# S4 kernel and context projections moved into earlier stages, answers and two norms in one stage, key shifts one group ahead

## The chip, the cores and the metric

The kernel runs on one core of a Trainium2 chip, with its five engines: TensorE (PE), VectorE (DVE), ScalarE (ACT), GpSimd (POOL) and SyncE (SP, which issues most transfers). The metric is the time of one execution in microseconds, the median of several runs.

## The reference

Two decoder layers on 8 sequences of 256 tokens with 256 features; each of six parts is added to x and followed by a norm.

```python
x = _layernorm(x + _L0_attn_ref(x, ...))             # selective scan
x = _layernorm(x + _L0_xattn_ref(x, ctx_768, ...))
x = _layernorm(x + _L0_ffn_ref(x, gate_w, w1, w2))   # 16 experts, one per token, 160 places each
x = _layernorm(x + _L1_attn_ref(x, ...))             # starts with layer_norm(x, ln1_scale, ln1_bias)
x = _layernorm(x + _L1_xattn_ref(x, ctx_768, ...))   # top 32 of the context, then an S4 convolution
x = _layernorm(x + _L1_ffn_ref(x, ...))              # product keys, 4096 experts
# of the expert part:   ans = einsum('tec,ecd->td', combine_weights, expert_out)
# of the top-32 part:   K = x_vision @ Wk;  V = x_vision @ Wv   (they depend on the context alone)
#   s4d:                K = 2 * einsum('dn,dnl->dl', dC, powers).real   (depends on weights alone)
# of the product keys:  q = (q - mean) * rsqrt(var + eps) * gamma + beta;  sim = q . keys
```

## The kernel before, in words

The 2048 tokens are 16 tiles of 128 rows in a buffer X, with a transposed copy XT. The kernel is a row of stages. Each stage is one block, in which every engine has a program of its own, written out in order and tied to the others by semaphores; between blocks all engines meet at a barrier. There is no scheduler. The order of the code is the order of each engine's queue, SP's and POOL's too.

**Routing** (`moe_route`, from L1359): TensorE makes the gate's logits and counts tokens by expert (L1423, L1424), VectorE ranks them and then computes small factors of the S4 kernel (`factor_step`), POOL scatters the 16 tiles to `moe_dispatch` in DRAM (L1489), ScalarE makes phases of the S4 tables.

**Experts** (`moe_experts`, L1494): for each of 16 experts TensorE does a first layer (L1573), turns the next expert's tokens (L1546) and the previous answers back (L1556), and a second layer (L1586). ScalarE and VectorE evacuate; SP loads weights two experts ahead and stores answers. Beside them ScalarE (`scalar_step`) and POOL (`gpsimd_program`) make the S4 tables UU and VV.

**Combine** (`norm_only` with `beside=Combine`): TensorE makes the S4 kernel as 256 products of UU and VV (L1312), VectorE copies it to KA (L1328), SP moves KA to KB in 16 transfers (L1305), TensorE transforms it (L1322) and VectorE copies the filter to KF (L1334). POOL gathers the experts' answers by token (L1291). VectorE adds them to X (L1298), behind its copies, and norms X (L442 to L450, L408).

**Performer** (`stage_performer`): a norm of X to X1 with the transposed copy in XT, a block in which POOL fills parts of VA with ones (L1735), then the projections (`products`, L204), where TensorE fills eight banks in turn and VectorE evacuates them. Later the inputs of the top-k attention are loaded (`topk_inputs`): context, weights, masks.

**Top-k attention** (`topk_attention`): projections of 4 query, 4 key and 16 value jobs (L204, copied by L238 and L239), with a norm of X beside them on VectorE and POOL (L362); then a block of two mask operations (L1998), then the attention.

**Product keys**: `norm_gram` norms X and accumulates a Gram matrix on TensorE (L2417), six tiles behind the turning (LAG); POOL centres its input (L2396). `peer_sides` handles 16 heads in 4 groups of 4. For a group, TensorE spreads the Gram matrix (L2524), VectorE accumulates variances (L2616) and makes scales, POOL scales keys (L2674), TensorE folds keys and shift (L2532, L2539), ScalarE copies, TensorE turns (L2548), ScalarE copies to WP (L2596). The shift is split into three bfloat16 rows BR by six operations of POOL (L2681 to L2686). Then come 8 units of 2 tiles: products of XT and WP and one of BR (L2562, L2563), which VectorE scans for the largest 8 (L2641, L2645). Groups 0 and 1 are accumulated ahead of the loop, group g + 2 in the loop of group g.

## Time and profile before

| | us |
|---|---|
| median of 3 runs | 2572.31 |
| lowest, highest | 2571.13, 2576.33 |
| the profiled execution's own time | 2596.7 |
| its span | 2594.9 |
| PE, DVE busy in the span | 2206.9 (85%), 1668.3 (64%) |
| ACT, POOL busy | 920.4 (35%), 884.3 (34%) |

The mean granted clock of TensorE is 0.925 of full speed. Matmuls are pipelined, so a busy share of PE is not the share of its peak. The page's own chain of waits (its part 4) follows the end of the program back through the last stage only, and shows 0% of the span for each engine, so the stages have to be read one at a time.

### The profile page before, as it was taken

How to read it: one execution, taken by the hardware profiler on the slowest of the kernel's cores; microseconds unless marked ns; L12 is line 12 of the kernel's file. 1: busy time of each engine (PE TensorE's matmuls, PEld its weight loads, DVE VectorE, ACT ScalarE, POOL GpSimd, SP SyncE). 2: the span in 40 equal slices, each digit the busy share in tenths (PEclk: the TensorE clock that was granted, in tenths of full speed). 3: DMA queues.
4: the chain of work that ended last, by engine and by line, in shares of the span. 5: the costliest groups of instructions: out<-in, count | busy, mean ns of one | idle time of the engine just before them, and what ended most of it. 6: DMA issues, size and time to landing. Idle time of an engine off the chain costs nothing. (4 is left out here: it accounts for less than half of the span.)

```text
span 2594.9 us, 34470 instructions
## 1 busy us (share of the span) xinstructions
PE 2206.9 (85%) x12574; PEld 1516.8 (58%) x12574; DVE 1668.3 (64%) x4342; ACT 920.4 (35%) x1840; POOL 884.3 (34%) x529
## 2 busy tenths in 40 slices
PE   8788888998964993898996777869778989999997
PEld 3355555634644992465473444325655678888886
DVE  6799999415662125456045999360547788888886
ACT  2498898215845210135312443023110222122220
POOL 0298887004508953132102333340421111111110
PEclk9899999999987996899997888879898999999998
DMA  3121111000033662100100000020030000000000
GB/s 98 54 70 49 50 49 37 11 0 1 1 116 116 231 222 61 49 2 2 39 21 19 1 1 1 0 87 25 1 130 1 3 1 1 1 1 1 1 1 33
DMA packets 59003, 103.07 MB, mean 40 GB/s; under 512 B 8082, under 2 KB 39698, under 8 KB 57684
## 3 DMA queue, kind: packets, MB, share of 16 engines
q1 hardware_dynamic: 57300, 96.69, 11.1%
q0 software_dynamic: 1536, 4.20, 0.5%
q8 instruction: 100, 1.64, 0.3%
q14 instruction: 67, 0.55, 0.1%
HBM read 91.04 MB, written 9.57 MB: 39 GB/s over the span
## 5 line engine op out<-in xcount | busy, mean ns | idle before, releaser
L762 POOL TENSOR_TENSOR XT<-mamba_DU,scan_BS 128x1024 f32<-128x1024 f32 x128 | 299.2, 2360 | 148.3 <-DMA scan_BS<-mamba_rows 110.8
L891 DVE TENSOR_TENSOR_SCAN scan_H<-scan_AB,XT 128x512 f32<-128x512 f32 x256 | 296.3, 1209 | 8.1 <-POOL XT L762 4.9
L2784 PE MATMUL ex_HP<-XT,pe_DOWN 128*128 128x256 f32 x1024 | 249.3, 390 | 5.8 <-PEq L2513 5.0
L2815 PE MATMUL ex_OP<-pe_UP,ex_GH 128*128 128x256 f32 x1024 | 231.5, 380 | 0.0
L2784 PEld LDWEIGHTS ex_HP<-XT,pe_DOWN 128*128 128x128 f32 x1024 | 194.0, 194 | 31.4 <-issue 5.1
L821 ACT ACTIVATE scan_AB<-mamba_E,mamba_AA 128x510 f32<-128x510 f32 x256 | 198.7, 776 | 37.9 <-DVE scan_H L891 33.5
L776 PEld LDWEIGHTS scan_TP<-ident,scan_H 128*128 128x128 f32 x1024 | 120.1, 142 | 157.3 <-DVE scan_H L891 81.2
L2845 ACT ACTIVATE ex_GH<-ex_HP 128x512 f32<-128x512 f32 x128 | 76.5, 599 | 380.4 <-PE ex_HP L2784 345.7
L2815 PEld LDWEIGHTS ex_OP<-pe_UP,ex_GH 128*128 128x128 f32 x1024 | 194.0, 190 | 26.1
L785 PE MATMUL scan_YT<-mamba_BC,ident 128*128 128x512 f32 x384 | 198.4, 599 | 4.1 <-ACT scan_YS L837 2.3
L776 PE MATMUL scan_TP<-ident,scan_H 128*128 128x128 f32 x1024 | 147.6, 278 | 46.0 <-DVE scan_H L891 46.0
L2871 POOL TENSOR_TENSOR ex_AS<-ex_AS,pe_IV 128x512 f16<-128x512 f16 x32 | 52.9, 1684 | 363.0 <-DVE ex_AS L2919 363.0
L2896 DVE TENSOR_TENSOR ex_L<-ex_IOTA,ex_KEYS 128x4096 f16<-128x4096 f16 x64 | 151.8, 2372 | 2.2
L830 ACT ACTIVATE mamba_BC<-scan_TP,scan_CT 128x512 f32<-128x512 f32 x192 | 129.6, 675 | 3.9 <-PE scan_TP L776 3.9
L2970 DVE SCALAR_TENSOR_TENSOR ex_GH<-ex_GP,ex_GH 128x1024 f32<-128x1024 f32 x64 | 78.4, 1225 | 61.0 <-issue 32.4
L1630 DVE TENSOR_SCALAR experts_HT<-experts_HP 128x320 f32<-128x320 f32 x32 | 15.7, 492 | 132.2 <-PE experts_HP L1573 132.2
L2562 PE MATMUL sides_SP_<-sides_WP,XT 128*128 128x256 f32 x256 | 79.8, 439 | 19.7 <-POOL sides_BR L2686 19.7
L2050 PE MATMUL tk_TP<-tk_DG,tk_PP 128*128 128x128 f32 x256 | 55.2, 403 | 47.3 <-ACT tk_DG L2143 47.3
L2804 PEld LDWEIGHTS ex_GP<-ex_R,ex_L 128*128 128x128 f16 x2048 | 77.8, 117 | 15.6 <-DVE ex_L L2896 4.7
L2050 PEld LDWEIGHTS tk_TP<-tk_DG,tk_PP 128*128 128x128 f32 x256 | 52.0, 311 | 54.9 <-ACT tk_DG L2143 54.9
L2804 PE MATMUL ex_GP<-ex_R,ex_L 128*128 128x32 f16 x2048 | 77.6, 191 | 7.5 <-DVE ex_L L2896 3.9
L1586 PE MATMUL experts_YT<-experts_HT,moe_W 128*128 128x160 f32 x512 | 76.2, 309 | 8.0 <-ACT experts_HT L1602 7.4
(452 smaller groups left out, 4553.6 us busy)
## 6 DMA issues: line engine op xcount, KB each, us to landing
moe_W<-in_L_ffn_w SPq DMA_DIRECT2D x32, 1024.0 KB, 7.5
scan_BS<-mamba_rows SPq DMA_DIRECT2D x64, 256.0 KB, 3.1
pe_DOWN<-in_L_ffn_down SPq DMA_DIRECT2D x1, 4096.0 KB, 12.3
pe_UP<-in_L_ffn_up SPq DMA_DIRECT2D x1, 4096.0 KB, 21.7
moe_dispatch<-s4t_BOTH SPq DMA_DIRECT2D x1, 2560.0 KB, 8.7
experts_XE<-moe_dispatch SPq DMA_DIRECT2D x16, 160.0 KB, 2.4
moe_answers<-experts_YE SPq DMA_DIRECT2D x16, 160.0 KB, 3.5
XT<-in_xT SPq DMA_DIRECT2D x4, 512.0 KB, 5.8
```

What stands on the lines that cost most here:

```text
L762: pool.tensor_tensor(BU[:, r % 2, cs], tokens(DU, cs, r // DS), row, ALU.mult).then_inc(bu_ready, 1)
L776: ins = pe.transpose(TP[:, i % SLOTS, c * P:(c + 1) * P], H[:, r % 2, c, tb * P:(tb + 1) * P], ident[:, 0:P])
L785: pe.matmul(YT[:, tb, :], ident[:, 0:P], HT[:, n % 4, :], start=(s == 0), stop=(s == DS - 1)).then_inc(y_added, 1)
L821: act.activation(later(AB[:, n % 2, :]), later(tokens(E, c, g)), ACT.Exp, scale=AA[:, 2 * c, s:s + 1], bias=AA[:, 2 * c, s:s + 1]).then_in ...
L830: act.activation(HT[:, n % 4, :], TP[:, item(r, tb) % SLOTS, :], ACT.Copy, scale=CT[:, TB * g + tb, s:s + 1]).then_inc(act_read, 1)
L891: v.tensor_tensor_scan(H[:, r % 2, c], AB[:, n % 2, :], BU[:, r % 2, c], 0.0, ALU.mult, ALU.add).then_inc(h_ready, 1)
L2050: ins = pe.matmul(TP[:, n % 2, 0, k * P:(k + 1) * P], PP[:, n % 2, h, k * P:(k + 1) * P], DG[:, h, :], start=(h == 0), stop=(h == XH - 1))
L2562: pe.matmul(SP_[:, n % BANKS, a, :], XT[:, k, t * P:(t + 1) * P], WP[:, k, keys], start=(k == 0), stop=False)
L2784: ins = pe.matmul(HP[:, n % 2, a, :], DOWN[:, k, 2 * q + a, :], XT[:, k, b * BLK:(b + 1) * BLK], start=(k == 0), stop=(k == KD - 1))
L2804: ins = pe.matmul(GP[:, n % 2, t, :], L[:, n % 2, t // RUN, :, t % RUN], R[:, n % 2, t // RUN, :, t % RUN], start=True, stop=True)
L2815: ins = pe.matmul(OP[:, m % 2, 0:D], GH[:, b % 2, j, a * P:(a + 1) * P], UP[:, j, :], start=(j == 0), stop=(j == J2 - 1))
L2896: v.tensor_tensor(L[:, n % 2], numbers(P), along(0, P), ALU.is_equal).then_inc(left_ready, 1)
```

## The change

The keys and values of the context (`ContextProducts`) are made in the routing, into space of the S4 tables, stored in DRAM during the experts and loaded as inputs of the top-k attention. ScalarE's two power steps move from behind experts 0 and 1 to behind experts 2 and 3, and wait for these stores. The S4 kernel is made in two chunks beside experts 14 and 15, four tiles of TensorE's columns at a time, two channels a product, and stored in DRAM (`s4_kernel`) in 16 transfers; the space for it on PSUM comes from YT, which has one bank instead of two. The combine stage and the performer's first norm become one (`combine_norms`), in groups of 2, 4, 4, 4 and 2 tiles; X1 is normed straight from the sum, by a variance with both epsilons, and X itself is normed by ScalarE beside the projections (`LateNorm`). The filter's transform is four more jobs of those projections. The Gram products go three tiles behind. In `peer_sides` the accumulation goes one group ahead, and the split of the shift is two copies on ScalarE and two operations on VectorE.

```diff
+class ContextProducts:
...
+    def tensor(self, pe):
+        self.loads.wait(pe)
+        for n in range(self.count):
+            if n >= self.RING:
+                pe.wait_ge(self.read, n - self.RING + 1)
+            bank = self.ring[:, n % self.RING, :]
+            if n < self.keys:
+                for k in range(2):
+                    ins = pe.matmul(bank, self.WK[0:KC[k], k, :], self.CT[0:KC[k], k, n * G4:(n + 1) * G4], start=(k == 0), stop=(k == 1))
+            else:
+                for a in range(2):
+                    t = 2 * (n - self.keys) + a
+                    for k in range(2):
+                        ins = pe.matmul(bank[:, a * D:(a + 1) * D], self.CT[0:KC[k], k, t * P:(t + 1) * P], self.WV[0:KC[k], k, :],
+                                        start=(k == 0), stop=(k == 1))
+            ins.then_inc(self.ready, 1)
+    def vector(self, v, first, last):
+        for n in range(first, last):
+            v.wait_ge(self.ready, n + 1)
+            bank = self.ring[:, n % self.RING, :]
+            if n < self.keys:
+                v.tensor_copy(self.KT[:, n * G4:(n + 1) * G4], bank).then_inc(self.read, 1)
+            else:
+                t = 2 * (n - self.keys)
+                v.tensor_copy(self.V[:, t:t + 2, :], bank.rearrange("p (a d) -> p a d", a=2)).then_inc(self.read, 1)
...
     def scalar_step(self, act, n):
-        if n == 1:
+        if n == 3:
+            act.wait_ge(self.space_free, 32)
             self.powers(act, self.HIGH, self.AR, ACT.Exp, LO).then_inc(self.moduli_ready, 1)
-        elif n == 2:
+        elif n == 4:
...
                 tables.load(sp)
+                context.loads.issue(sp)
                 sp.wait_ge(zero_ready, 1)
...
                 ch.link(v.tensor_tensor(WT[:], SM[:], KEEP[:], ALU.mult))
+                v.wait_ge(zeroed, 16)
+                context.vector(v, 0, 1)
                 for n in range(3):
                     tables.factor_step(v, n)
+                    context.vector(v, 2 * n + 1, 2 * n + 3)
+                context.vector(v, 7, context.count)
...
+                    if e == 1:
+                        sp.dma_start(io["topk_keys"], context.KT).then_inc(tables.space_free, 16)
+                        sp.dma_start(io["topk_values"], context.V).then_inc(tables.space_free, 16)
...
+                for n in range(CHUNKS):
+                    if n == CHUNKS - 1:
+                        store(NE - 2)
+                    sp.wait_ge(kernel_copied, n + 1)
+                    for j in range(TILES):
+                        for a in range(PAIR):
+                            r, d = j * KN + a * HI, n * P + j * KN + a * KI
+                            sp.dma_start(kernel[:, :, d:d + KI].rearrange("l h d -> h l d"), KA[r:r + HI, n, a]).then_inc(kernel_stored, 16)
                 store(NE - 1)
...
+                def kernel_products(n):
+                    pe.wait_ge(tables.factors_ready, 1)
+                    if n:
+                        pe.wait_ge(kernel_copied, n)
+                    for i in range(KI):
+                        for j in range(TILES):
+                            d = slice(n * P + j * KN + i * PAIR, n * P + j * KN + (i + 1) * PAIR)
+                            ins = pe.matmul(KP[j * KN:(j + 1) * KN, i * PAIR * LO:(i + 1) * PAIR * LO], tables.UU[:, d, :].rearrange("p a h -> p (a h)"),
+                                            tables.VV[:, d, :].rearrange("p a l -> p (a l)"), start=True, stop=True)
...
                         turn_back(e - 1)
+                    if e >= FIRST_CHUNK:
+                        kernel_products(e - FIRST_CHUNK)
                     pe.wait_ge(relu_act, 2 * (e + 1))
                     pe.wait_ge(relu_dve, 2 * (e + 1))
-                    if e >= 2:
-                        pe.wait_ge(ys_copied, e - 1)
+                    if e:
+                        pe.wait_ge(ys_copied, e)
...
+                def kernel_out(n):
+                    v.wait_ge(kernel_ready, n + 1)
+                    v.tensor_scalar(KA[:, n].rearrange("p a l i -> p i a l"), KP[:].rearrange("p (i a l) -> p i a l", a=PAIR, l=LO), 2.0, None, ALU.mult).then_inc(kernel_copied, 1)
...
+class LateNorm:
...
+    def scalar(self, act):
+        for t in range(NT):
+            act.activation(self.X[:, t, :], self.X[:, t, :], ACT.Identity, scale=self.RS[:, 0, t:t + 1], bias=self.NB[:, t:t + 1])
...
+def combine_norms(nc, name, late, X1, XT, ident, GA, ones, rest, scale, bias, loads, ahead):
...
+    GROUPS = (slice(0, 2), slice(2, 6), slice(6, 10), slice(10, 14), slice(14, 16))
...
+            @block.gpsimd
+            def _(pool):
+                for g in range(NG):
+                    for t in tiles(g):
+                        pool.indirect_dma_start(out=GA[:, t, :], out_offset=None, in_=rest.answers,
+                                                in_offset=bass.IndirectOffsetOnAxis(ap=rest.FROM[:, t:t + 1], axis=0)).then_inc(gathered[g], 16)
+                pool.memset(ones, 1.0)
+            @block.sync
+            def _(sp):
+                loads.issue(sp)
+                landed(sp, 2)
+                for a in ahead:
+                    a.issue(sp)
+            @block.vector
+            def _(v):
+                ch = Chain(v, dve_chain)
+                for g in range(NG + 1):
+                    if g < NG:
+                        landed(v, g)
+                        for t in tiles(g):
+                            ins = v.scalar_tensor_tensor(X[:, t, :], GA[:, t, :], rest.WT[:, t:t + 1], X[:, t, :], ALU.mult, ALU.add)
+                        ch.link(ins)
+                        for t in tiles(g):
+                            ins = v.bn_stats(raw[:, t, :], X[:, t, :])
+                        ch.link(ins)
+                        for t in tiles(g):
+                            ins = v.bn_aggr(MV[:, t, :], raw[:, t, :])
+                        ch.link(ins)
+                        v.tensor_scalar(RS[:, 0, GROUPS[g]], MV[:, GROUPS[g], 1], 1.0, 1e-5, ALU.mult, ALU.add)
+                        v.tensor_scalar(RS[:, 1, GROUPS[g]], MV[:, GROUPS[g], 1], 1.0 + 1e-6, 1e-11, ALU.mult, ALU.add).then_inc(var_ready, 1)
+                    if g:
+                        of = GROUPS[g - 1]
+                        v.wait_ge(std_ready, g)
+                        v.reciprocal(RS[:, :, of], RS[:, :, of]).then_inc(scale_ready, 1)
+                        v.wait_ge(scale_ready, g)
+                        for t in tiles(g - 1):
+                            v.tensor_scalar(X1[:, t, :], X[:, t, :], MV[:, t, 0:1], RS[:, 1, t:t + 1], ALU.subtract, ALU.mult).then_inc(normed, 1)
+                        v.scalar_tensor_tensor(NB[:, of], MV[:, of, 0], -1.0, RS[:, 0, of], ALU.mult, ALU.mult)
...
+                     (MASK[:], io["causal"]), (KEPS[:], io["L1_attn_key_eps"]), (WK_[:], io["dft_kernel"])] +
+                     [(KB[l * HI:(l + 1) * HI], inputs.kernel[l::LB].rearrange("i h d -> h i d")) for l in range(LB)])
...
+            for q in range(NF):
+                jobs.append((KF[:, q, :], [(WK_[:, i, q, :], KB[:, i, :]) for i in range(LO // LB)], by_channel))
+            products(nc, "pfproj", jobs, loads, dve_only=True, ahead=[mlp_loads], beside=late, evictor_needs=[loads])
             performer_core(nc, ident, QT, KT, VA, MASK, X1)
...
-                jobs.append((KT[:, tok], [(WK[0:KC[k], k, :], CT[0:KC[k], k, tok]) for k in range(2)], copy_out))
-            for t in range(NT):
-                jobs.append((V[:, t, :], [(CT[0:KC[k], k, t * P:(t + 1) * P], WV[0:KC[k], k, :]) for k in range(2)], copy_out))
             products(nc, "tkproj", jobs, inputs.loads, ahead=[film_loads], beside=NormBeside(nc, s2, X, Z, ident))
...
-    LAG = 6
+    LAG = 3
...
-                for c in range(2 * CG):
+                for c in range(CG):
...
-                        if g + 2 < NGR and u < ACCUMULATE_TO:
-                            spread((g + 2) * CG + u)
+                        if g + 1 < NGR and u < ACCUMULATE_TO:
+                            spread((g + 1) * CG + u)
...
+                    act.activation(B0[0:3, :], BP[0:3, 0:CK], ACT.Copy)
+                    act.activation(BH[0:3, 0, :], BP[0:3, 0:CK], ACT.Copy).then_inc(bias_copied, 1)
                     act.wait_ge(folded, g + 1)
                     act.activation(WT_[:, g % 2], WTP[:], ACT.Copy).then_inc(folded_copied, 1)
+                    act.wait_ge(rest_ready, g + 1)
+                    act.activation(BH[0:3, 1, :], BX[0:3, :], ACT.Copy).then_inc(rest_copied, 1)
                     act.wait_ge(turned, g + 1)
...
+                def bias_rest(g):
+                    v.wait_ge(bias_copied, g + 1)
+                    v.scalar_tensor_tensor(BX[0:3, :], BH[0:3, 0, :], SPLIT[0:3, 0:1], B0[0:3, :], ALU.mult, ALU.add).then_inc(rest_ready, 1)
+                def split_bias(g):
+                    v.wait_ge(rest_copied, g + 1)
+                    v.scalar_tensor_tensor(BR[0:3, g * CK:(g + 1) * CK], BH[0:3, 1, :], SPLIT[0:3, 1:2], BX[0:3, :], ALU.mult, ALU.add).then_inc(bias_split, 1)
...
-                def split_bias(g):
-                    b, x, h = B0[0:3, g % 2, :], BX[0:3, :], BH[0:3, :]
-                    pool.wait_ge(bias_copied, g + 1)
-                    for n in range(2):
-                        ch.link(pool.tensor_copy(h, b if n == 0 else x))
-                        if n == 0:
-                            ch.link(pool.tensor_scalar(x, h, SPLIT[0:3, 0:1], None, ALU.mult))
-                            ch.link(pool.tensor_tensor(x, b, x, ALU.subtract))
-                    ch.link(pool.tensor_scalar(b, h, SPLIT[0:3, 1:2], None, ALU.mult))
-                    pool.tensor_tensor(BR[0:3, g * CK:(g + 1) * CK], x, b, ALU.subtract).then_inc(bias_split, 1)
-                    pool.wait_ge(bias_split, g + 1)
```

VectorE's program from the end of the experts on, before. KA is the S4 kernel's copy, s_GA the gathered answers, RS the reciprocal deviations.

```order
L1328 TENSOR_SCALAR combine_KA<-combine_KP 16x32x16 x8
L1298 SCALAR_TENSOR_TENSOR X<-s_GA,moe_WT,X 128x256 x4
L442 BN_STATS moenorm_raw<-X 128x6 x4
L445 BN_AGGR moenorm_MV<-moenorm_raw 128x2 x4
L1298 SCALAR_TENSOR_TENSOR X<-s_GA,moe_WT,X 128x256 x4
L442 BN_STATS moenorm_raw<-X 128x6 x4
L445 BN_AGGR moenorm_MV<-moenorm_raw 128x2 x4
L450 RECIPROCAL moenorm_RS<-moenorm_RS 128x4
L408 TENSOR_SCALAR X<-X,moenorm_MV,moenorm_RS 128x256 x3
```

The same place of VectorE's program now. The gathered answers lie in pg_QT, pf_X is X1.

```order
L1807 SCALAR_TENSOR_TENSOR X<-pg_QT,rest_WT,X 128x256 x2
L1810 BN_STATS pfln_raw<-X 128x6 x2
L1813 BN_AGGR pg_MV<-pfln_raw 128x2 x2
L1815 TENSOR_SCALAR pg_RS<-pg_MV 128x2
L1816 TENSOR_SCALAR pg_RS<-pg_MV 128x2
L1807 SCALAR_TENSOR_TENSOR X<-pg_QT,rest_WT,X 128x256 x4
L1810 BN_STATS pfln_raw<-X 128x6 x4
L1813 BN_AGGR pg_MV<-pfln_raw 128x2 x4
L1815 TENSOR_SCALAR pg_RS<-pg_MV 128x4
L1816 TENSOR_SCALAR pg_RS<-pg_MV 128x4
L1820 RECIPROCAL pg_RS<-pg_RS 128x2x2
L1823 TENSOR_SCALAR pf_X<-X,pg_MV,pg_RS 128x256 x2
```

The eight copies of the kernel are gone from ahead of the first addition, and one pass of statistics serves both norms.

TensorE's program for the last two experts now. KP is the S4 kernel's bank; before, the same rows stand without the two of L1575.

```order
L1593 MATMUL experts_HP<-experts_XET,moe_W 128x160 x16
L1555 MATMUL experts_TP<-ident,experts_XE 128x80 x4
L1565 MATMUL experts_YP<-ident,experts_YS 80x128 x4
L1575 MATMUL experts_KP<-moe_VV,moe_UU 32x32 x64
L1608 MATMUL experts_YT<-experts_HT,moe_W 128x160 x16
L1593 MATMUL experts_HP<-experts_XET,moe_W 128x160 x16
L1565 MATMUL experts_YP<-ident,experts_YS 80x128 x4
L1575 MATMUL experts_KP<-moe_VV,moe_UU 32x32 x64
L1608 MATMUL experts_YT<-experts_HT,moe_W 128x160 x16
```

Two pieces of 64 products stand between the turning back and the second layer; before, 256 products stood behind the barrier.

POOL's program at the start of the sides, before (T is the shift, KS the scaled keys, B, BH and BX the parts of the split, IV the kept indices).

```order
L2695 MEMSET sides_ONE 128x128
L2671 COPY sides_T<-sides_SHIFT 128x12
L2674 TENSOR_TENSOR sides_KS<-sides_KEYS,sides_SCALE 128x256
L2671 COPY sides_T<-sides_SHIFT 128x12
L2674 TENSOR_TENSOR sides_KS<-sides_KEYS,sides_SCALE 128x256
L2681 CAST sides_BH<-sides_B 3x256
L2683 TENSOR_SCALAR sides_BX<-sides_BH,sides_SPLIT 3x256
L2684 TENSOR_TENSOR sides_BX<-sides_B,sides_BX 3x256
L2681 CAST sides_BH<-sides_BX 3x256
L2685 TENSOR_SCALAR sides_B<-sides_BH,sides_SPLIT 3x256
L2686 TENSOR_TENSOR sides_BR<-sides_BX,sides_B 3x256
L2692 CAST pe_IV<-sides_I 128x2x32 x5
```

POOL's program there now.

```order
L2843 MEMSET sides_ONE 128x128
L2831 COPY sides_T<-sides_SHIFT 128x12
L2834 TENSOR_TENSOR sides_KS<-sides_KEYS,sides_SCALE 128x256
L2840 CAST pe_IV<-sides_I 128x2x32 x5
L2831 COPY sides_T<-sides_SHIFT 128x12
L2834 TENSOR_TENSOR sides_KS<-sides_KEYS,sides_SCALE 128x256
L2840 CAST pe_IV<-sides_I 128x2x32 x8
```

The six operations of the split are gone from POOL, and the second group's keys are scaled in the loop.

## Rows read from the trace of the kernel before

**Rows 1.** Tiles s_GA and combine_KA: count, ns min/median/max, first and last start.

```profile
L1291 POOL DMA_INDIRECT s_GA<-moe_answers,moe_FROM x16: 945/949/1067, 977.8 to 996.7; - x16
...
L1328 DVE TENSOR_SCALAR combine_KA<-combine_KP x8: 1002/1021/1023, 984.9 to 1010.7; 16x512 f32<-16x512 f32 x8
```

**Rows 2.** Timeline, combine to projections: start, us, instruction, idle before it.

```profile
1000.48 10.23 PE L1312 MATMUL combine_KP<-s_VV,s_UU 128*16 128x16 f32 x390 [1.21 <-issue]
...
1011.60 1.64 DVE L1298 SCALAR_TENSOR_TENSOR X<-s_GA,moe_WT,X 128x256 f32<-128x256 f32 x4
...
1030.51 1.40 DVE L1334 COPY KF<-combine_KP 128x256 f32<-128x256 f32 x4
...
1033.88 1.40 DVE L442 BATCH_NORM_STATS2 pfln_raw<-X 128x6 f32<-128x256 f32 x4 [1.96 <-PEq L3013]
...
1054.95 9.72 PE L204 MATMUL pfproj_ring<-XT,pg_WQ 128*128 128x512 f32 x16 [6.10 <-PEq L1732]
```

**Rows 3.** Windows: length, busy PE, PEld, DVE, ACT, POOL, clock, DMA.

```profile
985.00:1000.00 15.00, 2.31 (x27) 1.62 (x28) 0.92 (x1) 0.00 (x0) 9.62 (x11) 0.50 0.34 98
...
1918.00:2035.00 117.00, 100.20 (x402) 61.83 (x400) 92.14 (x787) 5.11 (x11) 20.83 (x53) 0.90 0.00 1
```

**Rows 4.** Timeline, projections of the top-k attention.

```profile
1361.77 9.94 POOL L362 TENSOR_SCALAR s_Z<-X,tl_norm_MV,tl_norm_RS 128x256 f32<-128x256 f32 x8 [119.57 <-DVE tl_norm_RS L373]
...
1370.75 2.07 PE L204 MATMUL tkproj_ring<-topk_CT,topk_WK 128*128 128x512 f32 x4
...
1372.75 20.15 PE L204 MATMUL tkproj_ring<-topk_WV,topk_CT 128*128 128x256 f32 x64
...
1393.68 1.23 DVE L1998 TENSOR_SCALAR tk_TM<-topk_M 128x2048 f32<-128x2048 uint8 x1 [0.32 <-PEq L187]
```

**Rows 5.** Timeline, sides ahead of the loop.

```profile
1903.60 0.61 POOL L2674 TENSOR_TENSOR sides_KS<-sides_KEYS,sides_SCALE 128x256 f32<-128x256 f32 x1
...
1906.33 1.08 PE L2539 MATMUL sides_WTP<-sides_WQT,sides_KS 128*64 128x256 f32 x8
...
1908.80 0.60 ACT L2596 ACTIVATE sides_WP<-sides_TP 128x512 f32<-128x512 f32 x1 [0.74 <-PE sides_TP L2548]
...
1913.52 2.04 PE L2562 MATMUL sides_SP_<-sides_WP,XT 128*128 128x256 f32 x4 [4.75 <-POOL sides_BR L2686]
```

**Rows 6.** Waits in the loop of the sides: us in total, times, longest.

```profile
DVE pe_SV L2641 <- PE sides_SP_ L2563: 22.5, 5, 6.8
```

**Rows 7.** Timeline, routing to experts.

```profile
774.32 1.06 PE L1424 MATMUL route_CS<-route_RUN,route_TRI 128*128 128x256 f32 x2
...
785.12 0.96 POOL L1489 DMA_INDIRECT moe_dispatch<-X,moe_TO  x1 [0.30 <-issue]
...
802.08 16.60 SPq L1527 DMA_DIRECT2D experts_XE<-moe_dispatch  x3
```

**Rows 8.** Timeline, last expert.

```profile
968.17 4.58 PE L1586 MATMUL experts_YT<-experts_HT,moe_W 128*128 128x160 f32 x32 [0.19 <-issue]
...
973.95 0.69 DVE L1621 COPY experts_YE<-experts_YP 80x512 f32<-80x512 f32 x1 [5.25 <-PE experts_YP L1556]
```

**Rows 9.** Tile pfcore_A: ns min/median/max, first and last start.

```profile
L1834 PEld LDWEIGHTS pfcore_OP<-pfcore_A,pg_VA x256: 106/107/110, 1130.6 to 1194.8; 128*32 128x32 f32 x128
```

**Rows 10.** DMA queue of the page: packets, MB, share of 16 engines.

```profile
q1 hardware_dynamic: 57300, 96.69, 11.1%
```

**Rows 11.** Timeline, VectorE in the norm of the combine stage.

```profile
1019.75 1.66 DVE L1298 SCALAR_TENSOR_TENSOR X<-s_GA,moe_WT,X 128x256 f32<-128x256 f32 x4
...
1023.36 1.22 DVE L408 TENSOR_SCALAR X<-X,moenorm_MV,moenorm_RS 128x256 f32<-128x256 f32 x3
...
1024.50 1.66 DVE L1298 SCALAR_TENSOR_TENSOR X<-s_GA,moe_WT,X 128x256 f32<-128x256 f32 x4
```

**Rows 12.** Timeline, end of the Gram matrix.

```profile
1882.46 2.50 POOL L2396 TENSOR_TENSOR s_FO<-X,s4norm_ROW 128x512 f32<-128x512 f32 x2
...
1887.07 6.26 PE L2417 MATMUL s4norm_GP<-s_FO 128*128 128x258 f32 x28
```

**Rows 13.** Tile sides_JUNK: ns min/median/max, first and last start.

```profile
L2616 DVE SCALAR_TENSOR_TENSOR sides_JUNK<-sides_AT,sides_WQT x16: 410/414/417, 1897.3 to 1965.7; 128x256 f32<-128x256 f32 x16
```

282 lines of the change are left out of this document (149 added, 133 removed).

## The prediction

> **What bounds the kernel now.** The page's busy row says little: TensorE is busy most of the span, but every place that the change touches is a stretch in which it waits or issues slowly. The chain of waits covers only the last stage. So I read the timeline at the joints of the stages, then the tiles whose buffers move, then single stretches.
>
> The first place is the step behind the experts. There TensorE makes the S4 kernel in 512 tiny products, VectorE copies them out in 8 copies, and only then does VectorE add the experts' answers, which GpSimd gathers meanwhile. The reader is to see that the gathers run from 977.8 to 996.7 [rows 1], but the first answer is added at 1011.60 [rows 2], behind the eighth copy [rows 1]: the answers lie there for some 13 us. A window shows why the copies are late: between 985 and 1000 TensorE ran 27 records, and from 1000.48 it ran 390 in 10.23 us [rows 2, 3], and its idle time is put down to issue, not to an engine. Then come norm, transform, a barrier, the next norm, a fill on GpSimd, another barrier, and at 1054.95 the projections. From the first gather to there it is 77.1 us.
>
> The second is the projection stage of the top-k attention: 16 value products in a row take 20.15 us on TensorE while POOL's share of the norm is done after 9.94 us [rows 4]. The third is the scoring of the keys (the sides): its first product starts at 1913.52 and waits for POOL's last piece of the split shift [rows 5]; in the loop VectorE waits for TensorE 22.5 us in 5 waits, the longest 6.8 [rows 6], although it is busy only 92.14 of 117 us [rows 3]. Those long waits stand where a group of heads ends and the next group's split shift isn't there.
>
> **Part by part**, against the profiled execution's own 2596.7 us (span 2594.9; it lies 24.4 above the median of the runs, 2572.3).
>
> *Context products in the routing: +6.* Added on TensorE behind the counting product (ends 775.4 [rows 7]): 4 key products of 2.0 us (1372.75 less 1370.75) and 16 value products of 20.15/16 = 1.26 [rows 4], together 28.1: 803.5. VectorE's 12 copies (4 of 256 columns take 1.40 [rows 2], so 0.7 each) stand between its factor steps, and TensorE has four banks only; I give its waits for them 2, and the last copy ends at 806. With the barrier (1.9 us elsewhere: the last copy of the filter begins 1030.51 and takes 1.40, the next stage begins 1033.88 [rows 2]) the experts start at 808 where they started at 802.08 [rows 7]. Bounds: 0 (if it hides under the scatters) and +12 (if every bank wait is paid). The six context loads go ahead of the zero fill of the dispatch rows on SP and on the rings; the scatters wait for these zeros only behind the whole ranking of experts, so I cost that at nothing, and if the zeros come late, each us of it lies on the path. The stores of keys and values (3 MB) go ahead of the third expert's weights on SP, which are asked for later, after the first expert: nothing. The two 7 us steps of ScalarE (powers) move from experts 0 and 1 to 2 and 3 with the same stall: nothing.
>
> *Kernel products beside experts 14 and 15: +11.5.* Twice 64 products with 32 columns, 128 records, in front of the second layer, where TensorE is never late (W2 of the last expert starts right behind, 968.17 [rows 8]): they are all on the path. The nearest row is 390 records in 10.23 us, 26 ns each with 16 columns [rows 2], 3.4 us a chunk; the far one is the 107 ns of a 128x32 weight load [rows 9], 14 a chunk. With twice the columns I take 40 ns, 5 a chunk, 10 in all. The copy-out is off the path. Then SP: 8 stores of a chunk, each of 256 pieces of 64 B, stand ahead of the last answers. The mean packet of this kernel costs 11.1% of 16 x 2594.9 over 57300 = 80 ns [rows 10]; 128 pieces per engine are then 10 us against the 7.5 that the second layer and its copies need anyway. I take 1.5 more; bounds 0 and 5. The Trainium skill ("DMA: Bandwidth & Descriptors", Specifications) names 512 B as the smallest transfer at line rate and says that below it the engine reads, modifies and writes. No row here isolates such a store, so by that rule this term is nearer its upper bound or over it, and the sum some 4 us less of a gain.
>
> *Answers, norm and next norm in one stage: -42.3.* 77.1 becomes: 4.3 until the first two gathers have landed (two issues at about 1.2 and 2 for the transfer), then VectorE's work. A group of four tiles takes it 4.74 us now (1019.75 to 1024.50), with three of four scalings (1.22) on it [rows 11]; now four, and three small operations: 5.5, so 22 for 16 tiles. Groups 2 and 3 land just behind it: 4.2 of waiting. The last group's scaling, transpose and copy: 2.4; barrier 1.9. Sum 34.8. GpSimd's fill of ones, a block of its own before, lies beside the last groups. Bounds: 29 (gathers alone, 20, their tail and barrier) and 50 (if nothing starts before the last gather).
>
> *Filter transform among the projections: +3.4.* 4 products of 4 records; nothing hides them, since TensorE bounds the projections. Products of this width with one short operand take 1.26 [rows 4]; the full operands here should be no slower, and I take 0.85, two thirds; bounds 2 and 5. The late norm on ScalarE lies beside 70 us of products and costs nothing.
>
> *Top-k projections: -21.6.* Four products remain, done by 1363. What ends last is POOL's 8 scalings, 1361.77 + 9.94 = 1371.7, and the next block, now at 1393.68, starts 0.4 later [rows 4]. Bounds -19 and -22.
>
> *Gram three tiles behind: -5.* The tail is 28 records, 6.26 us, from 1887.07; POOL's last centering ends at 1882.46 + 2.50 = 1884.96 [rows 12]. With two tiles' products behind that it would end at 1887; TensorE starts colder, so I take 5 of 6. Bounds 0 and -7.
>
> *Sides, before the loop: -6.* Keys are scaled at 1904.2; folding, its copy, the turn and its copy take 1906.33 to 1909.40, 3.1 us; so products can start at 1907.5 instead of 1913.52 [rows 5]. Bounds -4 and -7. *In the loop: -13.* VectorE's 92.1 grows by one group's four accumulations (0.41 each and two short reads [rows 13], 0.6 in all) and some 14 operations of 0.2 to 0.3, an estimate, to 98; the 22.5 of waiting becomes three waits of about 1.5 (TensorE now waits at the fold for the scales, some 2 us, and is ahead by no more). 98 + 6 = 104 for 117. Bounds 0 (the fold takes the place of the split) and -18.
>
> Sum: 6 + 11.5 - 42.3 + 3.4 - 21.6 - 5 - 6 - 13 = -67. 2596.7 becomes 2529.7, and from the median 2572.3 - 67 = **2505**.
>
> **Rivals.** *Slow issue under the gathers (2518).* Between 985 and 1000, with 11 gathers running, TensorE issued 27 records with nothing to wait for [rows 3]. If that slowness hits VectorE and TensorE in the new stage, they begin when the last gather is out: 20 + 22 + some 6 = 48, 13 more. For: the row. Against: few instructions are needed there. The Trainium skill ("Runtime: NRT & Kernel Launch", Instruction fetch mechanics) says a taken branch forces a fetch of its page; the trace has such a branch at each stage's start, and only this one is followed by slow issue.
>
> *VectorE holds up the gathers (2515).* In the new stage VectorE works while GpSimd issues. If each gather waits out two of its 0.41 us scalings (three take 1.22 [rows 11]), 16 gathers take 13 us more, of which 10 show. Against: in the routing a scatter's issue took 0.96 beside a working VectorE [rows 7], as the gathers' 0.95 beside an idle one [rows 1]. The Trainium skill ("SBUF — State Buffer", SBUF: two separate sides) has VectorE's two-port operations lock GpSimd out of writing descriptors; by that rule this rival would be the forecast, and the rows speak against it.
>
> *The fold takes the split's place (2518).* TensorE waits for the scales longer than the 2 us, its clock falls, and the next group starts late as now; the loop keeps its 117. Against: TensorE is only one or two units ahead there.
>
> *Slower than before (2578).* The 64 B stores are the one piece without a row. All engines wait for them at the end of the experts. They decide once a piece takes (67 + 1.5 + 7.5)/128 = 0.59 us on its engine; at 0.64 us, 128 of them are 82 us, and the kernel ends near 2578. Against: 80 ns is the mean packet [rows 10].
>
> *More gain (2490).* Gathers bound the new stage (-6), records of 32 columns cost 26 ns (-3), the loop gains 18 (-5).
>
> **How the numbers follow.** Forecast (2495 to 2512) 0.52, slow issue 0.11, held gathers 0.09, fold 0.11, more gain 0.12, slower 0.03, and 0.02 for a loss that eats the gain just about. Two of these terms can add up, to 2530. The range 2482 to 2535 leaves out the last two and the far ends. A measurement of this kernel tells 0.2% (5 us) from no change, and all but those two lie beyond it: faster 0.95, same 0.02, slower 0.03.
>
> **What would show it.** Right: the first answer is added about 5 us after the first gather, the projections start 33 to 37 us after it; the top-k stage's mask step follows POOL's scalings; in the sides no wait of VectorE is over 2.5 us; the experts start near 808; experts 14 and 15 take 5 us more each. Wrong: record gaps put down to issue in the new stage, kernel stores that land over 5 us after the last answers, or a fold that TensorE waits for longer than 3 us.

## The result and the profile after

The changed kernel takes 2528.85 us (median of 4 runs, 2521.45 to 2534.71), the kernel before 2571.72 beside it (4 runs, 2570.64 to 2576.33): the ratio is 0.9819, 95% interval 0.9801 to 0.9836. That is faster, clear of the noise, by 43 us between the medians and 46 by the ratio, where 67 was forecast. The time lies 24 us above the 2505 of the forecast, inside its range of 2482 to 2535 and outside the likeliest case's own 2495 to 2512.

The two profiled executions say something else: 2596.7 before, 2528.31 after, 68.4 us apart. So stage by stage the forecast can be read from the traces, and the 24 us are a matter of the level (2572 or 2597) from which it was subtracted. Both are told below. The execution of 2596.7 is not one of the four timed runs beside it.

The new stage comes first. This is its timeline after (start, duration, engine, line, operation, count, idle time before and what ended it), to be held against [rows 1, 2]:

```profile
985.65 0.30 SPq L1520 DMA_DIRECT2D moe_answers<-experts_YE  x1
...
989.78 1.06 POOL L1789 DMA_INDIRECT pg_QT<-moe_answers,rest_FROM  x1 [31.01 <-POOLq L3160]
...
993.92 0.88 DVE L1807 SCALAR_TENSOR_TENSOR X<-pg_QT,rest_WT,X 128x256 f32<-128x256 f32 x2 [8.30 <-DMA pg_QT<-moe_answers,rest_FROM]
...
998.99 1.67 DVE L1807 SCALAR_TENSOR_TENSOR X<-pg_QT,rest_WT,X 128x256 f32<-128x256 f32 x4 [2.85 <-DMA pg_QT<-moe_answers,rest_FROM]
...
1004.14 1.67 DVE L1807 SCALAR_TENSOR_TENSOR X<-pg_QT,rest_WT,X 128x256 f32<-128x256 f32 x4 [0.37 <-DMA pg_QT<-moe_answers,rest_FROM]
...
1010.02 3.52 POOL L1791 MEMSET pg_VA<- 128x4096 f32 x1
1012.90 1.67 DVE L1807 SCALAR_TENSOR_TENSOR X<-pg_QT,rest_WT,X 128x256 f32<-128x256 f32 x4 [3.31 <-DMA pg_QT<-moe_answers,rest_FROM]
...
1018.21 0.88 DVE L1807 SCALAR_TENSOR_TENSOR X<-pg_QT,rest_WT,X 128x256 f32<-128x256 f32 x2
...
1026.37 9.78 PE L204 MATMUL pfproj_ring<-XT,pg_WQ 128*128 128x512 f32 x16 [2.29 <-PEq L1784]
```

The first answer is added 4.1 us after the first gather (forecast 4.3), and the first projection starts 1026.4 - 989.8 = 36.6 us after it (forecast 34.8, 77.1 before). A group of four takes VectorE 5.3 (1012.90 to 1018.21; forecast 5.5). One row was not foreseen: at 1012.90 VectorE has waited 3.3 us for the fourth group. The windows around it (busy us and counts of PE, PEld, DVE, ACT, POOL, then granted clock, DMA share, GB/s) have the DMA engines full:

```profile
1000.00:1005.00 5.00, 1.12 (x4) 0.67 (x4) 4.49 (x19) 1.06 (x4) 3.93 (x4) 0.50 0.39 107
1005.00:1010.00 5.00, 1.40 (x7) 1.37 (x8) 4.45 (x19) 1.53 (x5) 3.94 (x4) 0.50 0.88 297
1010.00:1015.00 5.00, 0.57 (x3) 0.17 (x1) 2.07 (x6) 2.23 (x7) 3.54 (x2) 0.50 1.02 341
```

The last two experts, with the two pieces of kernel products (L1575), against [rows 8]:

```profile
962.08 4.61 PE L1593 MATMUL experts_HP<-experts_XET,moe_W 128*128 128x160 f32 x32
...
967.34 1.30 PE L1575 MATMUL experts_KP<-moe_VV,moe_UU 128*32 128x32 f32 x128
...
968.57 4.62 PE L1608 MATMUL experts_YT<-experts_HT,moe_W 128*128 128x160 f32 x32
...
972.89 4.40 PEld L1593 LDWEIGHTS experts_HP<-experts_XET,moe_W 128*128 128x128 f32 x32
```

From one first layer to the next it is 10.9 us where a steady expert takes 9.56: a piece costs 1.3, not 5. Each single record still reads about 0.2 us long:

```profile
L1575 PEld LDWEIGHTS experts_KP<-moe_VV,moe_UU x256: 105/109/114, 967.3 to 979.0; 128*32 128x32 f32 x128
L1575 PE MATMUL experts_KP<-moe_VV,moe_UU x256: 195/197/218, 967.3 to 979.0; 128*32 128x32 f32 x128
```

128 of them in 1.30 us are 10 ns apiece. The columns after the count are ns min, median and max of one record, which says how long a record lasts and nothing of how many are under way at once.

The stores of the kernel and their time to landing; the transform among the projections (count, then busy us and mean ns); the top-k projections, POOL's scalings and the mask step, against [rows 4]:

```profile
L1541 SPq DMA_DIRECT2D s_kernel<-moe_TT x16: 302/450/1404, 969.7 to 984.0; - x16
...
DMA to landing us min/median/max: 1.7/1.8/2.8
```

```profile
L204 PE MATMUL pfproj_ring<-pg_KB,pg_WK_ 128*128 128x256 f32 x16 | 3.6, 379 | 0.0
```

```profile
1329.31 8.51 PE L204 MATMUL tkproj_ring<-XT,topk_first_WQ 128*128 128x512 f32 x16 [1.71 <-PEq L3160]
...
1336.57 9.91 POOL L362 TENSOR_SCALAR s_Z<-X,tl_norm_MV,tl_norm_RS 128x256 f32<-128x256 f32 x8 [119.48 <-DVE tl_norm_RS L373]
...
1346.82 1.23 DVE L2147 TENSOR_SCALAR tk_TM<-topk_first_M 128x2048 f32<-128x2048 uint8 x1 [5.67 <-PEq L187]
```

No store takes over 2.8 us. The mask step follows POOL's last scaling (1346.48) by 0.3 us.

In the sides, VectorE's waits and then TensorE's (in total, times, longest), against [rows 6]:

```profile
DVE pe_SV L2790 <- PE sides_SP_ L2714: 11.6, 5, 3.4
```

```profile
PE sides_BP L2683 <- POOL sides_T L2831: 8.6, 4, 2.6
```

The waits are halved, from 22.5 to 11.6, but the longest is 3.4 where at most 2.5 was forecast, and TensorE now waits at the fold.

By stage, from the first records of neighbouring stages in the two traces:

| stretch | before | after | difference | forecast |
|---|---|---|---|---|
| start to the routing's first product | 757.8 | 759.0 | +1.2 | 0 |
| to the first expert | 46.8 | 50.7 | +3.9 | +6 |
| to the first gather | 173.2 | 180.1 | +6.9 | +11.5 |
| to the first projection | 77.1 | 36.6 | -40.5 | -42.3 |
| to the performer's core | 72.4 | 75.9 | +3.5 | +3.4 |
| to the top-k projections | 227.2 | 227.0 | -0.2 | 0 |
| to the top-k stage's first weighting (tk_TP) | 61.5 | 39.9 | -21.6 | -21.6 |
| to the Gram's first transpose | 451.4 | 449.4 | -2.0 | 0 |
| to the sides' first product | 46.1 | 37.1 | -9.0 | -11 |
| to the last stage's first product | 124.6 | 115.3 | -9.3 | -13 |
| to the end of the span | 556.8 | 555.5 | -1.3 | 0 |

Each column is one execution. Other traces of the kernel before, told below, tell how far one varies: there the stretch to the first weighting takes 59.9 to 61.6 us and the one to the Gram's first transpose 446.5 to 451.4. So -21.6 is good to some 2 us, and the -2.0 below it tells nothing.

### The profile page after: what moved, and what is told of

It is laid out like the page before. It is cut to its first block and busy times, and to the rows that moved or that the text cites. A ratio compares the mean times of both kernels' runs of the same rounds, so it can differ in the third digit from the quotient of the medians.

```text
span 2526.5 us, 33894 instructions
## 1 busy us (share of the span) xinstructions
PE 2182.5 (86%) x12318; PEld 1497.9 (59%) x12318; DVE 1658.0 (66%) x4318; ACT 925.3 (37%) x1851; POOL 858.5 (34%) x497
## 5 line engine op out<-in xcount | busy, mean ns | idle before, releaser
L1656 DVE TENSOR_SCALAR experts_HT<-experts_HP 128x320 f32<-128x320 f32 x32 | 15.7, 492 | 135.7 <-PE experts_HP L1593 135.7
L2199 PE MATMUL tk_TP<-tk_DG,tk_PP 128*128 128x128 f32 x256 | 47.5, 361 | 48.2 <-ACT tk_DG L2292 48.2
L2948 PEld LDWEIGHTS ex_GP<-ex_R,ex_L 128*128 128x128 f16 x2048 | 77.8, 117 | 15.7 <-issue 5.4
L1608 PEld LDWEIGHTS experts_YT<-experts_HT,moe_W 128*128 128x128 f32 x512 | 74.4, 200 | 10.3 <-ACT experts_HT L1624 8.2
L2038 POOL TENSOR_TENSOR pfcore_A<-pfcore_A,pg_MASK 128x512 f32<-128x512 f32 x32 | 40.5, 1267 | 115.5 <-ACT pfcore_A L2018 115.5
```

Of the source, the lines that this page charges most:

```text
L1608: ins = pe.matmul(YT[:, k * CAP:(k + 1) * CAP], W2[:, e % 2, c, k * P:(k + 1) * P], HT[:, e % 2, c, :], start=(c == 0), stop=(c == NHID - 1))
L2948: ins = pe.matmul(GP[:, n % 2, t, :], L[:, n % 2, t // RUN, :, t % RUN], R[:, n % 2, t // RUN, :, t % RUN], start=True, stop=True)
```

## The experiments

**The level of the kernel before.** *before_again* is the kernel before, unchanged.

> The kernel before, unchanged. The two profiles on hand differ by 68.4 us (2596.7 against 2528.3), the timed runs by some 43 (medians 2571.7 and 2528.9). Theory A: the 24 us above its median belong to that one execution of the kernel before, in one or a few places; a new profile is then near 2572, and beside the old one it shows the place. Theory B: being profiled costs this kernel 24 us in the stages that the change removes (the slow issue beside the gathers, the long top-k projections), so the new profile is again near 2596 and its timed runs near 2572. The timed ratio to itself is 1.000 either way.

Measured: 2594.44 (10 runs), and 2594.8 for the 25 runs of the kernel before beside it; its profiled execution took 2589.8. Neither theory held as put: the traced execution is no slower than the others, and on this occasion every run of the kernel before, traced or not, is near 2595, as the first traced execution was. On the occasion on which the change was timed it was at 2572. So the question became what the changed kernel does at the upper level. *after_again* is the changed kernel, unchanged.

> The changed kernel, unchanged, on a second occasion. The kernel before has run at two levels: 2571.7 (where the change was timed) and 2594.8 (ten more runs and a profile, on another occasion; its stages there agree with the first profile within a few us). Theory A: the change is worth the sum of its stages, 67 to 68 us, wherever the kernel before runs at 2595, so this one runs at 2527, and at 2572 it is worth only 43 because 24 us of what it removes do not arise there. Theory B: the level shifts both kernels alike, the gain is 43 to 46 on either, and this one runs at 2550 where the one before runs at 2595 (2528 where it runs at 2572).

Measured: 2525.34 against 2594.32, ratio 0.9739 (0.9725 to 0.9752): 69.0 us. Theory A holds. The medians of the changed kernel are 2529 and 2525 on the two occasions; only the kernel before has two levels. The record names chip 10 for the occasion of before_again, chip 12 for this one and chip 10 for the third, and none for the first. So the upper level was met on two chips, and whether the four runs at 2572 were made on another is not known. *before_third*, the kernel before once more on the third occasion, was to show a profile at the lower level.

> The kernel before once more, for its level: 2572 in the four runs beside the changed kernel, 2594 to 2595 in 34 runs on two later occasions. If it comes at 2572 here, the profile shows where the 23 us lie: theory A says in the stage that combines the answers (the products there no longer slowed by the gathers, 10 to 15 us) and one other place that the change removes. If it comes at 2595, nothing new.

Measured: 2597.36, beside 14 runs with a median of 2596.12. So no trace of the lower level exists.

**The parts one by one.** *lag3*, on the kernel before:

```diff
-    LAG = 6
+    LAG = 3
```

> The kernel before with the Gram products three tiles behind the norm where they were six behind. The prediction's term: 5 us less (2567), bounds 0 and 7. Rival: TensorE starts colder and the tail costs the same, 2572; or it waits for VectorE and POOL more often in the middle, 2575.

Measured: 2593.44 against 2594.8, ratio 0.9995 (0.9986 to 1.0004). The times don't tell it from no change. In its trace the stretch from the Gram's first transpose to the sides' first product is 43.3 where before_again has 46.0: 2.7 us, half the term.

*sides_alone*, on the kernel before:

```diff
-                for c in range(2 * CG):
+                for c in range(CG):
...
-                ch = Chain(pool, pool_chain)
...
+                bias_rest(0)
+                split_bias(0)
```

> The kernel before with the new scoring stage of the keys alone (keys one group ahead, shift split by ScalarE and VectorE). Between the two profiles on hand the loop became 9.7 us shorter and what stands before it, with the Gram's tail, 9.1. Theory (the prediction's terms -6 and -13, as the two profiles show them): 15 to 19 us less, 2553 to 2557, and no wait of VectorE over 3.5 us in the loop. Rival: the 6.8 us waits at the ends of a group in the old profile are themselves part of the 24 us by which that execution stood above the median; then the gain is 0 to 8, 2564 to 2572.

Measured: 2577.44, ratio 0.9931 (0.9917 to 0.9946), 17.4 us. The theory holds: the waits at the ends of a group are no accident of one execution.

*moved_alone*, on the kernel before: kernel products beside experts 14 and 15, and the one stage for answers and both norms.

```diff
+                    if e >= FIRST_CHUNK:
+                        kernel_products(e - FIRST_CHUNK)
...
+            late = LateNorm(s1, X)
...
+            products(nc, "pfproj", jobs, loads, dve_only=True, ahead=[mlp_loads], beside=late, evictor_needs=[loads])
```

> The kernel before with two parts of the change alone: the kernel products beside experts 14 and 15, and answers, norm and next norm in one stage with the filter transform among the projections. Routing, top-k stage, Gram and sides are those of before. By the two profiles: 2.5 us for the products, about 3 for stores and what else the experts lose, 40.6 less from first gather to first projection, 3.6 for the transform: 32 less than before on the same chip. Rival: the 10.4 us that VectorE waits there for nothing on record (beside the gathers) is a fetch of code that comes back in the new stage: 22 less. If context alone (7.7), sides (17.4), Gram (1.4) and this add up, the whole change is worth 58 where the kernel before runs at 2595; if theory A is right about 67, the parts must help each other.

Measured: 2561.45, ratio 0.9874 (0.9859 to 0.9889), 32.9 us. The theory holds to a us, the rival fails.

*context_alone*, on the kernel before: keys and values of the context made in the routing.

```diff
+                context.tensor(pe)
...
+                        sp.dma_start(io["topk_keys"], context.KT).then_inc(tables.space_free, 16)
+                        sp.dma_start(io["topk_values"], context.V).then_inc(tables.space_free, 16)
```

> The kernel before with the context's keys and values made in the routing and loaded in the top-k stage; the kernel products, the combining stage and the rest as they were. Between the two profiles the experts start 5.1 us later and the top-k scoring starts 21.6 us earlier than what precedes it. Theory: 16.5 us less, 2555. Rival: the 24 us of surplus lie in the top-k projections or the loads before them, and the gain is 0 to 5, 2567 to 2572.

Measured: 2587.1, ratio 0.997 (0.9958 to 0.9983), 7.7 us: between the two. The top-k stage gave 20.0 against before_again (39.9 for 59.9). The loss is in the routing, where the experts' first product comes at 818.1, 13.0 later than in before_again; in the changed kernel it comes at 809.7. Its timeline there:

```profile
797.64 0.68 DVE L1176 COPY s4t_BOTH<-route_ring 128x512 f32<-128x512 f32 x1
...
800.96 0.96 POOL L1548 DMA_INDIRECT moe_dispatch<-X,moe_TO  x1 [0.30 <-issue]
804.44 2.48 DVE L1176 COPY s4t_BOTH<-route_ring 128x512 f32<-128x512 f32 x4 [6.12 <-remote]
805.19 9.27 PE L1164 MATMUL route_ring<-route_WV,s4t_TT 128*128 128x256 f32 x16 [2.60 <-DVE s4t_BOTH L1176]
```

VectorE stood 6.1 us for nothing on record ("remote": no engine and no transfer of the trace ended the wait), with products ready to be copied. TensorE ran out of banks and stood 2.6 us, and its next 16 records took 9.27 us, 0.58 each, where the 64 of the changed kernel take 20.15 in a row, 0.31 each. The windows show the granted clock fall from 1.00 to 0.58:

```profile
786.00:802.00 16.00, 16.00 (x51) 7.22 (x49) 11.88 (x25) 15.69 (x32) 12.27 (x13) 1.00 0.48 177
802.00:815.00 13.00, 9.86 (x18) 4.18 (x18) 3.68 (x6) 0.00 (x0) 0.00 (x0) 0.58 0.03 10
```

Once TensorE had stopped, most of the next 13 us were granted at the lower level, 1.2 GHz.

The changed kernel has the same stop of VectorE, only shorter: 5.0 us in after_again, 3.7 in late_loads, 2.2 in scale3, 1.9 (put down to issue) in *both*, and none in its first trace. The rows of after_again:

```profile
784.88 20.15 PE L1151 MATMUL route_ring<-route_WV,moe_TT 128*128 128x256 f32 x64
...
801.66 2.48 DVE L1163 COPY moe_BOTH<-route_ring 128x512 f32<-128x512 f32 x4 [5.00 <-remote]
```

There the banks last: TensorE's 64 records go on in one row, and the stop costs nearly nothing.

The four parts add up to 59.4, the whole to 69.0. *no_context* is the changed kernel with the context back in the top-k stage; it asks where the 9.6 between them are.

> The changed kernel with the context's keys and values made in the top-k stage again (as before), all else as changed. Measured one by one against the kernel before, at its 2594: context 7.7 us less, sides 17.4, Gram 1.4, kernel products and combining stage 32.9; together 59.4, the whole change 69.0. Theory: context alone was hit by something that the rest of the change takes away (VectorE stood 6.1 us in the routing for nothing on record, then TensorE ran at the lower clock, and the stage began 2.6 us later), so it is worth 15 to 18 in the changed kernel: this one runs at 2541 to 2543. Rival: context is worth 8 there too and the surplus of 9.6 lies between the other parts: 2533.

Measured: 2541.91 against 2596.12, ratio 0.9802 (0.9785 to 0.9819), where the changed kernel has 0.9739 on the occasion before: 16.6 us by the medians, 0.0063 (16.4 us) by the ratios, and 14.8 if each is first held against the kernel before beside it. The theory's time holds, the rival's does not. The context's part is worth 15 to 17 in the changed kernel and 7.7 alone. Not because the stop is gone there, as the theory has it: it is there too and is covered by the banks. From the routing's first product to the first expert context_alone takes 57.3 us and the changed kernel 50.7; TensorE's 2.6 us without a bank and the 4.2 that its last 16 records lost account for these 6.6. Why the stop is a little longer in the one program is not shown.

**What slowed the old combining stage.** *gathers_after*, on the kernel before:

```diff
     def gather(self, pool):
+        pool.wait_ge(self.k_copied, D // self.DB)
```

> The kernel before with one wait more: GpSimd starts the 16 gathers of the answers only when VectorE has copied out all 8 pieces of the S4 kernel. Disputed: why TensorE issued 27 records in the 15 us beside the gathers, and VectorE stood 10.4 us for nothing on record. Theory (the gathers in flight slow the issue on both): without them the 512 products and 8 copies take about 15 us in place of 34, the gathers follow, the answers are added as they land, and the kernel is 8 to 12 us faster, 2583 to 2587 where the kernel before runs at 2595, though a wait was added. Rival (the stage's code comes in slowly whatever else runs): the copies still end 34 us after the stage starts and the gathers come on top: 3 to 8 us slower.

Measured: 2585.86 against 2596.12, ratio 0.9964 (0.995 to 0.9977): a wait more, and 10.3 us less. The products and VectorE's waits for them without gathers in flight, and then the same of the kernel before on the first of these occasions:

```profile
L1313 PE MATMUL combine_KP<-s_VV,s_UU x512: 176/176/190, 978.9 to 993.2; 128*16 128x16 f32 x171
...
L1329 DVE TENSOR_SCALAR combine_KA<-combine_KP x8: 1002/1017/1024, 980.7 to 993.4; 16x512 f32<-16x512 f32 x8
```

```profile
DVE combine_KA L1329 <- PE combine_KP L1313: 10.0, 8, 4.3
```

```profile
L1312 PE MATMUL combine_KP<-s_VV,s_UU x512: 176/184/208, 977.9 to 1011.5; 128*16 128x16 f32 x171
...
L1328 DVE TENSOR_SCALAR combine_KA<-combine_KP x8: 1002/1020/1026, 985.8 to 1011.7; 16x512 f32<-16x512 f32 x8
```

```profile
DVE combine_KA L1328 <- PE combine_KP L1312: 18.8, 7, 15.1
DVE combine_KA L1328 <- remote: 10.4, 1, 10.4
```

The same 512 products take 14.3 us in place of 33.6, and the "remote" wait is gone from the copies. (One of 1.7 us stands later, at VectorE's norm, just behind the last gather.) So it takes the gathers to slow both engines; the stage's code alone does not. Whether it is GpSimd's issuing or the transfers, and whether they act through the fetch of code, was not taken apart.

**Two waits of the changed kernel.** *scale3*:

```diff
-    ACCUMULATE_TO, SCALE_AT, FOLD_AT, TURN_AT, SPLIT_AT = CG, CG, 5, 6, 6
+    ACCUMULATE_TO, SCALE_AT, FOLD_AT, TURN_AT, SPLIT_AT = CG, CG - 1, 5, 6, 6
```

> The changed kernel with the scales of the next group of keys one unit of tiles earlier (SCALE_AT 3 for 4), in front of VectorE's fourth scan. In the profile after, TensorE waits 2.0 us at each of three folds for them, and VectorE then 1.4 and 3.3 us at the ends of a group. Theory: these waits go, 3 to 6 us less than the changed kernel. Rival: VectorE now waits for ScalarE's root in the middle instead and TensorE is bound by its banks anyway: within 1 us.

Measured: 2517.42, ratio to the kernel before 0.9715 (0.9697 to 0.9733), against 0.9739 for the changed kernel on the same occasion; 7.9 us by the medians. The intervals overlap, the traces do not: the loop takes 115.3 us in after, after_again and late_loads, and 106.9 in scale3 and *both*. VectorE's waits in the sides, after_again and then scale3:

```profile
DVE pe_SV L2790 <- PE sides_SP_ L2714: 11.6, 5, 3.4
```

```profile
DVE pe_SV L2790 <- PE sides_SP_ L2714: 3.3, 1, 3.3
```

And a window over the sides of each, in the same order:

```profile
1850.00:1960.00 110.00, 102.45 (x427) 64.52 (x427) 95.17 (x790) 7.65 (x19) 10.41 (x36) 0.95 0.09 39
```

```profile
1854.00:1956.00 102.00, 97.53 (x428) 62.02 (x428) 95.01 (x793) 7.53 (x19) 10.41 (x36) 1.00 0.10 42
```

The loop is 8.4 us shorter, with the same work of VectorE, and TensorE keeps its full clock. More than the theory's 3 to 6.

*late_loads*:

```diff
                 loads.issue(sp)
-                landed(sp, 2)
+                landed(sp, 3)
```

> The changed kernel with the projections' weights and the stored kernel asked for after the fourth group of gathers instead of the third. In the profile after, VectorE waits 3.3 us for the fourth group (1009.6 to 1012.9) while the 16 DMA engines are full from 1005 to 1013 with these loads. Theory: the gathers land on time, 3 us less than the changed kernel. Rival: the loads then end behind the first projection and TensorE waits for them: 0 to 4 us more.

Measured: 2523.41, ratio 0.9724 (0.9711 to 0.9738): 1.9 us by the medians, unclear from the times alone. VectorE's waits in the new stage, after_again and then late_loads:

```profile
DVE X L1807 <- DMA pg_QT<-moe_answers,rest_FROM: 15.3, 4, 8.3
```

```profile
DVE X L1807 <- DMA pg_QT<-moe_answers,rest_FROM: 11.6, 3, 8.3
```

The wait of the fourth group is gone (3.7 us), and first addition to first projection is 29.9 us for 32.9. TensorE did not wait for the loads.

*both* joins the two edits.

> The changed kernel with both edits of the last experiments: scales one unit earlier (it gave 7.9 less) and loads after the fourth group of gathers (1.9 less by the medians, 3.1 less between first answer and first projection by the profiles). They touch different stages; theory: the gains add, 2515 where the changed kernel runs at 2525. Rival: late loads give nothing that holds: 2517.

Measured: 2516.19 against 2596.12, ratio 0.9703 (0.9687 to 0.972). It is the fastest of all by the ratio, 79.9 us under the kernel before and better than the changed kernel beyond both intervals. What late_loads adds to scale3 (0.9703 against 0.9715) can't be told from the times, and its trace shows no gain: first addition to first projection is 33.3 us here. The fourth group's answers were in time, but VectorE came late itself. One scaling of the third group lasted 4.25 us where the others take 0.41, beside GpSimd's fill of ones:

```profile
1007.04 5.23 DVE L1823 TENSOR_SCALAR pf_X<-X,pg_MV,pg_RS 128x256 f32<-128x256 f32 x4 [0.40 <-DVE pg_RS L1820]
...
1008.58 3.54 POOL L1791 MEMSET pg_VA<- 128x4096 f32 x1
```

```profile
L1823 DVE TENSOR_SCALAR pf_X<-X,pg_MV,pg_RS x16: 405/412/4252, 1001.4 to 1021.8; 128x256 f32<-128x256 f32 x16
```

The scaling and the fill end within 0.2 us of each other. The same is in the trace of scale3 (4.26 us), whose loads are not late, and so its list of waits reads 11.6, 3, 8.3 as well. In the other traces no scaling meets the fill. So what late_loads gives hangs on where the fill falls; a fill placed elsewhere was not tried.

## Why the prediction was right, and where not

*The level: wrong, and all of the miss.* The step of the prediction that failed is "2596.7 becomes 2529.7, and from the median 2572.3 - 67 = 2505". The first half was right to 1.4 us (2528.31 measured). The second took the 24.4 between the trace and the median for a surplus of that execution, to be found alike in both kernels. In 59 later runs the kernel before took 2588.5 to 2601.5; the changed kernel was at 2528.85 on the first occasion and at 2525.34 on a later one. So, if both kernels ran under the same conditions on the first occasion, what tells the two levels apart lies in something that the change removes. gathers_after shows one such thing, worth 10.3 us of the 24: the slowing beside the gathers, which goes though not one operation is taken out. That it was absent at 2572 is a guess: no trace of that level exists, the chip of those four runs is not on record, and the cause stays open.

*Two pieces of luck.* The sum of the stages came out to 1.4 us because its errors cancel: kernel products and context cost 6.7 less than forecast, the sides' loop gave 3.7 less, the new stage 1.8, and one execution of a kernel differs from the next by some 5. And 2528.85 lies inside the range only because its upper part was kept for slow issue, held gathers and a late fold, none of which made these 24 us.

*Answers and both norms: right* (-40.5 for -42.3). VectorE bounds the stage as worked out. The missing 2 us are in the waits behind the first group, 6.5 for the forecast 4.2. Of these 3.3 are the fourth group's, behind weight loads for which the DMA engines were full; late_loads took it away. The prediction gave the loads that collide with it no term, and none to the fill of ones, which held VectorE up for 3.8 us in scale3 and *both*.

*Kernel products: right in kind, mis-sized.* +6.9 for +11.5, of which the products are 2.6, for 10. The failed step is "I take 40 ns": I scaled up from a row of 16 columns, 26 ns each, and bounded by the length of one weight load. That row was not a slowed one: without gathers, in gathers_after, 171 such records take 4.64 us, 27 ns each. But its records all go to one column group of the array; here, dealt to four in turn, they cost 10 ns each. That the dealing does it was not tested by itself. The rest is 1.0 between the last copy of answers and the first gather (4.85 for 3.86), 1.7 by which ScalarE's two steps of 7 us delay the experts behind them more than before (14.4 and 15.8 us from first layer to first layer, before 12.9 and 15.7; "nothing" in the prediction), and 1.6 of other waits, of which one of 1.2 for an expert's weights is in this trace alone. From before_again to after_again the stretch grows by 4.4 only.

*64 B stores, and with them the slower rival: fallen.* They land in 1.7 to 2.8 us, and the last store of answers, issued behind them, in 2.0 as before. What the Trainium skill ("DMA: Bandwidth & Descriptors", Specifications) says of transfers under 512 B does not show here: eight stores of 32 KB a piece of the kernel, none on the path.

*Context in the routing: right in the changed kernel* (+3.9 for +6, and -21.6, where the tenth is luck), but only there. Alone it cost +10.4 from the routing's start and +13.0 from the program's, at the bound of +12. The prediction had waits for banks as that bound, but no stop of VectorE and no fall of the clock behind it.

*Top-k, transform: right.* POOL's scalings end last, as said; 3.5 for 3.4.

*Gram: mis-sized* (2.7 for 5, by lag3). *Sides: right in sign, short by a third in the loop* (-9.3 for -13). The failed step is "the 22.5 of waiting becomes three waits of about 1.5", for which the sum has 6: it became five waits, 11.6 in all. VectorE's own work grew as said (100.3 us busy in the loop for 94.8, by 5.5 for 6), and TensorE's three waits at the fold were 2 us each, as said (6.0 in after_again). But VectorE then waited 8.3 for TensorE in four places (11.6 less the first 3.3, which scale3 has too): the fold's wait was paid again. The rival (the fold takes the split's place) was right that the wait comes back and the clock falls (0.95), and wrong about the size: the loop did not keep its 117. scale3 removes the wait and gets what was missing.

*Slow issue under the gathers: fallen for the new stage.* Few instructions run there and none is late. But the reading of [rows 3] was right that the gathers slow others in the old stage: gathers_after shows it. The Trainium skill's account of code fetch ("Runtime: NRT & Kernel Launch", Instruction fetch mechanics) alone does not give it, since the same stage with the same branch at its start is fast once the gathers are out of the way.

*VectorE holds up the gathers: fallen.* The window 1000 to 1005 of the trace after has VectorE busy 4.49 of 5 us, and the gathers' median is 946 ns (949 before):

```profile
L1789 POOL DMA_INDIRECT pg_QT<-moe_answers,rest_FROM x16: 942/946/1189, 989.8 to 1009.0; - x16
```

The lock that the Trainium skill ("SBUF — State Buffer", SBUF: two separate sides) describes, between VectorE's two-port operations and GpSimd, does not show with the gathers; one of 16 took 1.19. It fits what scale3 and *both* show the other way round: a scaling of VectorE lasts 4.25 us beside GpSimd's fill and ends with it. By the records that scaling began 0.6 us before the fill, so the order in which they took the lock is not shown.

## What to carry to other kernels

Before you subtract a sum from a median, make sure that the trace and the median belong to the same level; if they are 1% apart, the forecast has two values, and the change may remove the very thing that makes them differ. A wait that an engine pays once in a loop may be paid again by its consumer, and by the clock: issue what it waits for one step earlier before you count the gain as taken. A part measured alone is not its worth in the whole: the context's part was worth 7.7 us alone and 15 to 17 with the rest. A stop costs nothing while the buffers behind it last (5.0 us with four banks) and more than itself once they don't (6.1). And look for a gain in every trace that should have it: late_loads took 3.0 us off the new stage, and *both*, with the same edit, took off none.
